# A gated recurrence with its 256 pairs of time steps written out, turned into a loop on each engine that holds two pairs, with the transfers cut to one pair each

## The reference

```python
Xz = einsum('btc,hc->tbh', X, Wxz) + bxz      # and Xr, Xh in the same way
def step(H, xs):
    Z = sigmoid(xz + H @ Whz.T + bhz)
    R = sigmoid(xr + H @ Whr.T + bhr)
    H_tilda = tanh(xh + R * H @ Whh.T + bhh)
    H_new = Z * H + (1.0 - Z) * H_tilda
    Y = H_new @ Whq.T + bhq
    return (H_new, Y)
return x + transpose(Ys)
```

## Time and profile before

| | |
|---|---|
| time, median of 3 runs | 2449.64 us (2446.89 to 2451.39) |
| profiled execution, its own time | 2457.01 us |
| its span, first to last instruction | 2455.2 us |
| TensorE matmul busy | 2351.4 us (96%) |
| TensorE weight load busy | 2230.2 us (91%) |
| VectorE busy | 1345.5 us (55%) |
| ScalarE busy | 817.1 us (33%) |
| instructions in the trace | 177755 |
| mean granted TensorE clock | 0.998 |

### The profile page before, as it was taken

The page is one execution under the profiler, slowest core; times in us unless marked ns, Lnnn a source line. Parts: engine busy times, 40 slices in busy tenths (PEclk is TensorE's granted clock), DMA queues, the critical chain, the costliest instruction groups (busy, mean ns, idle before and its releaser), DMA issues.

```text
span 2455.2 us, 177755 instructions
## 1 busy us (share of the span) xinstructions
PE 2351.4 (96%) x81984; PEld 2230.2 (91%) x81984; DVE 1345.5 (55%) x8961; ACT 817.1 (33%) x4610; POOL 0.8 (0%) x6
## 2 busy tenths in 40 slices
PE   8999999999999999999999999999999999999999
PEld 7999989999999999899999899989999898988898
DVE  3555555555555555555555555555555555555555
ACT  2333333333333333333333333333333333333333
POOL 0000000000000000000000000000000000000000
PEclk9999999999999999999999999999999999999999
DMA  4000000000000000000000100000000000000000
GB/s 165 30 22 22 22 30 30 30 13 22 30 30 30 13 30 22 30 30 13 30 22 30 30 23 21 22 30 30 30 13 22 30 30 30 13 22 30 30 13 13
DMA packets 16491, 69.53 MB, mean 28 GB/s; under 512 B 2304, under 2 KB 2432, under 8 KB 14848
## 3 DMA queue, kind: packets, MB, share of 16 engines
q1 hardware_dynamic: 15744, 58.17, 6.7%
HBM read 41.39 MB, written 16.78 MB: 24 GB/s over the span
## 4 chain that ended last, share of the span: by engine, by line
PE 95%; issue 4%; DMA 1%; SPq 0%; DVE 0%; ACT 0%
PE pre L180 57%; PE pre L147 29%; PE y_bank L159 9%; DMA wh<-in_w_hh 1%; SPq L110 0%; SPq L112 0%; DVE pre_t L269 0%; DVE fresh L305 0%; SPq L118 0%; DVE reset_state L294 0%; ACT cand L258 0%; SPq L116 0%; ACT z_not L254 0%; DVE states L309 0%; DVE kept L299 0%
## 5 line engine op out<-in xcount | busy, mean ns | idle before, releaser
L180 PE MATMUL pre<-wh,states 128*16 128x128 f32 x32768 | 1093.4, 273 | 22.7 <-issue 13.4
L147 PE MATMUL pre<-wx,xt 128*32 128x128 f32 x24576 | 1034.6, 273 | 67.9 <-issue 63.7
L269 DVE STREAM_TRANSPOSE pre_t<-pre 128x32 f32<-128x32 f32 (+2 forms) x3584 | 618.4, 216 | 801.8 <-PE pre L180 767.1
L180 PEld LDWEIGHTS pre<-wh,states 128*16 128x16 f32 x32768 | 949.9, 104 | 68.3 <-issue 60.8
L147 PEld LDWEIGHTS pre<-wx,xt 128*32 128x32 f32 x24576 | 814.3, 110 | 120.0 <-issue 117.2
L180 PE MATMUL pre<-wh,reset_state 128*16 128x128 f32 (+1 forms) x16384 | 616.8, 273 | 6.9 <-issue 5.5
L251 ACT ACTIVATE r_gate<-pre_t 128x16 f32<-128x16 f32 (+1 forms) x1536 | 234.5, 215 | 1003.1 <-DVE pre_t L269 1003.1
L180 PEld LDWEIGHTS pre<-wh,reset_state 128*16 128x16 f32 (+1 forms) x16384 | 473.0, 103 | 29.3 <-issue 27.8
L258 ACT ACTIVATE cand<-pre_t 128x16 f32<-128x16 f32 (+1 forms) x1536 | 234.8, 215 | 327.6 <-DVE pre_t L269 327.6
L159 PE MATMUL y_bank<-wq,states 128*32 128x128 f32 x8192 | 299.7, 273 | 1.5 <-DVE states L309 1.5
L159 PEld LDWEIGHTS y_bank<-wq,states 128*32 128x32 f32 x8192 | 258.0, 110 | 1.8 <-DVE states L309 1.8
(11 more groups left out here) (11 smaller groups left out, 10.5 us busy)
## 6 DMA issues: line engine op xcount, KB each, us to landing
xt<-in_x_t SPq DMA_DIRECT2D x32, 512.0 KB, 3.4
y_io<-in_x_res SPq DMA_DIRECT2D x32, 512.0 KB, 3.3
out<-y_io SPq DMA_DIRECT2D x32, 512.0 KB, 2.8
wx<-in_w_xr SPq DMA_DIRECT2D x1, 1024.0 KB, 5.8
wx<-in_w_xz SPq DMA_DIRECT2D x1, 1024.0 KB, 6.0
wx<-in_w_xh SPq DMA_DIRECT2D x1, 1024.0 KB, 8.2
wh<-in_w_hr SPq DMA_DIRECT2D x1, 1024.0 KB, 11.0
wh<-in_w_hz SPq DMA_DIRECT2D x1, 1024.0 KB, 12.9
```

The costliest lines, as they stand in the source:

```text
L147: mm = nc.tensor.matmul(pre[k % 2][Q * j:Q * (j + 1), g, 0:P], xt[:, n % 2, tp, m, :], wx[g][:, m, P * j:P * (j + 1)], start=False, stop=( ...
L180: mm = nc.tensor.matmul(pre[k % 2][Q * j:Q * j + rows, g, 0:P], of, wh[g][:, m, P * j:P * (j + 1)], start=False, stop=(m == G - 1), skip_g ...
L269: nc.vector.transpose(flat(pre_t[g][:, a:b]), pre[k % 2][:, g, Q * a:Q * b]).then_inc(done, 1)
```

## The change

Each engine's program becomes a hardware loop (`Fori`) whose body is one turn: pairs 2i and 2i+1. The first turn is written out ahead of the loop and the last one behind it, so the loop runs over i = 1 to 126. Semaphores still count up through the whole kernel, so a wait inside the loop is against a value worked out from the loop's register (`k = 2 * i + par`, `t = 2 * k + s`). Buffer halves are chosen by `par`, which is a constant in the body. The transfers of `xt`, `y_io` and `out` are now one pair each (64 KB instead of 512 KB), with their addresses in the chip's main memory worked out from the loop's register. The work on TensorE, VectorE and ScalarE and its order are the same.

```diff
+        def pair_loop(eng, pair):
+            for par in range(2):
+                pair(0, par, first=True, last=False)
+            with eng.Fori(1, turns - 1) as i:
+                for par in range(2):
+                    pair(i, par, first=False, last=False)
+            for par in range(2):
+                pair(turns - 1, par, first=False, last=True)
@@ sync @@
+            def pair(i, par, first, last):
+                k = 2 * i + par
+                if not last:
+                    sp.wait_ge(xt_used, k + 1)
+                    load_xt(k + 2, par)
+                if not (first and par == 0):
+                    sp.wait_ge(y_added, k)
+                    sp.dma_start(out[k - 1], y_io[:, 1 - par]).then_inc(stored[1 - par], 16)
+                    if not (last and par == 1):
+                        sp.wait_ge(stored[1 - par], 16 * (i + par))
+                        load_res(k + 1, 1 - par)
-            for n in range(tiles):
-                if n + 2 < tiles:
-                    sp.wait_ge(xt_used, n + 1)
-                    load_xt(n + 2)
-                sp.wait_ge(y_added, PAIRS * (n + 1))
-                sp.dma_start(out[n], y_io[:, n % 2]).then_inc(stored[n % 2], 16)
-                if n + 2 < tiles:
-                    sp.wait_ge(stored[n % 2], 16 * (n // 2 + 1))
-                    load_res(n + 2)
@@ tensor @@
-                if tp == PAIRS - 1 and g == H and end == G:
+                if g == H and end == G:
                     mm.then_inc(xt_used, 1)
+            def pair(i, par, first, last):
+                k = 2 * i + par
+                more = not (last and par == 1)
+                start = first and par == 0
+                recur(R, 2 * k, par, 0, start)
+                recur(Z, 2 * k, par, 0, start)
+                if more:
+                    pe.wait_ge(xt_loaded[1 - par], 16 * (i + 1 + par))
+                    pe.wait_ge(pre_filled, k + 2)
+                    project_x(1 - par, R, 0, 1)
+                recur(H, 2 * k, par, 0, start)
...
@@ vector @@
+            def add_y(k, par, loads):
+                dve.wait_ge(y_loaded[par], 16 * loads)
                 dve.wait_ge(y_projected, k + 1)
```

More of the change, by code:

```diff
@@ L24, in gru @@
 def gru(nc, x_t, x_res, h0, w_x, w_h, w_q, b_gate, b_out, out):
-    tiles = x_t.shape[0]
-    pairs = tiles * PAIRS
+    pairs = x_t.shape[0]
+    turns = pairs // 2
     with ExitStack() as ctx:
@@ L92, in flat, with state_of, load_xt, load_res @@
             return t.rearrange("p m b -> p (m b)")
-        def state_of(k, s):
-            return states[:, (k + 1) % 2, :, 2 * B:3 * B] if s == 0 else states[:, k % 2, :, B:2 * B]
+        def state_of(par, s):
+            return states[:, 1 - par, :, 2 * B:3 * B] if s == 0 else states[:, par, :, B:2 * B]
+        def pair_loop(eng, pair):
[6 more added lines that the diff above has]
+                pair(turns - 1, par, first=False, last=True)
         @block.sync
         def _(sp):
[L100 to L106, removed]
+            def load_xt(k, par):
+                sp.dma_start(xt[:, par], x_t[k]).then_inc(xt_loaded[par], 16)
+            def load_res(k, par):
+                sp.dma_start(y_io[:, par], x_res[k]).then_inc(y_loaded[par], 16)
+            def pair(i, par, first, last):
[9 more added lines that the diff above has]
+                        load_res(k + 1, 1 - par)
+            load_xt(0, 0)
             sp.dma_start(wx[R][:], w_x[R]).then_inc(wx_loaded[R], 16)
@@ L119, in _ @@
             sp.dma_start(wq[:], w_q).then_inc(wq_loaded, 16)
-            load_res(0)
-            load_xt(1)
-            load_res(1)
-            for n in range(tiles):
-                if n + 2 < tiles:
-                    sp.wait_ge(xt_used, n + 1)
-                    load_xt(n + 2)
-                sp.wait_ge(y_added, PAIRS * (n + 1))
-                sp.dma_start(out[n], y_io[:, n % 2]).then_inc(stored[n % 2], 16)
-                if n + 2 < tiles:
-                    sp.wait_ge(stored[n % 2], 16 * (n // 2 + 1))
-                    load_res(n + 2)
-            for n in range(2):
-                sp.wait_ge(stored[n], 16 * (tiles // 2))
+            load_xt(1, 1)
+            load_res(0, 0)
+            load_res(1, 1)
+            pair_loop(sp, pair)
+            sp.wait_ge(y_added, pairs)
+            sp.dma_start(out[pairs - 1], y_io[:, 1]).then_inc(stored[1], 16)
+            for par in range(2):
+                sp.wait_ge(stored[par], 16 * turns)
         @block.gpsimd
@@ L183, in recur @@
                 mm.then_inc(pre_done[g], 1)
+            def pair(i, par, first, last):
[9 more added lines that the diff above has]
+                recur(H, 2 * k, par, 0, start)
+                if not start:
+                    if first:
+                        pe.wait_ge(wq_loaded, 16)
+                    project_y(k - 1, 1 - par)
+                if more:
+                    project_x(1 - par, R, 1, G)
+                recur(R, 2 * k + 1, par, 1)
+                recur(Z, 2 * k + 1, par, 1)
+                if more:
+                    project_x(1 - par, Z, 0, 1)
+                recur(H, 2 * k + 1, par, 1)
+                if more:
+                    project_x(1 - par, Z, 1, G)
+                    project_x(1 - par, H, 0, G)
             pe.wait_ge(zeroed, 2)
@@ L199, in _, with fill_pre, fill_y, pair @@
                 project_x(0, g, 0, G)
[L201 to L225, removed]
+            pair_loop(pe, pair)
             for h in range(N):
                 pe.wait_ge(state_ready[h], 2 * pairs + 1)
-            project_y(pairs - 1)
+            project_y(pairs - 1, 1)
         @block.scalar
         def _(act):
[L232 to L237, removed]
+            def fill_pre(par):
+                nc.scalar.copy(pre[par][:, :, 0:P], bias_rows[:]).then_inc(pre_filled, 1)
+            def fill_y(k, par, first):
+                if not first:
                     act.wait_ge(y_added, k - 1)
[L239 to L245, removed]
+                nc.scalar.copy(y_bank[par][:, 0:P], bias_out[:]).then_inc(y_filled, 1)
+            def pair(i, par, first, last):
+                k = 2 * i + par
                 for s in range(2):
@@ L260, in _, with turn, pair @@
                     if s == 0:
-                        fill_y(k)
-                    elif k + 2 < pairs:
-                        fill_pre(k + 2)
+                        fill_y(k, par, first)
+                    elif not last:
+                        fill_pre(par)
+            act.wait_ge(bias_ready, 1)
+            act.wait_ge(banks_primed, 1)
+            fill_pre(0)
+            fill_pre(1)
+            pair_loop(act, pair)
         @block.vector
         def _(dve):
-            def turn(g, k, part, done):
+            def turn(g, par, part, done):
                 a, b = part
[L269 to L274, removed]
+                nc.vector.transpose(flat(pre_t[g][:, a:b]), pre[par][:, g, Q * a:Q * b]).then_inc(done, 1)
+            def add_y(k, par, loads):
+                dve.wait_ge(y_loaded[par], 16 * loads)
                 dve.wait_ge(y_projected, k + 1)
-                nc.vector.tensor_tensor(y_io[:, n % 2, tp, :], y_bank[k % 2][:, 0:P], y_io[:, n % 2, tp, :], ALU.add
+                nc.vector.tensor_tensor(y_io[:, par, :], y_bank[par][:, 0:P], y_io[:, par, :], ALU.add
                                         ).then_inc(y_added, 1)
[L279 to L284, removed]
+            def pair(i, par, first, last):
+                k = 2 * i + par
                 for s in range(2):
                     t = 2 * k + s
-                    old, new = state_of(k, s), state_of(k + s, 1 - s)
+                    old, new = state_of(par, s), state_of(par if s == 0 else 1 - par, 1 - s)
                     dve.wait_ge(pre_done[R], t + 1)
                     for h in range(N):
-                        turn(R, k, PARTS[h], r_turned[h])
+                        turn(R, par, PARTS[h], r_turned[h])
                     for h, (a, b) in enumerate(PARTS):
@@ L296, in _ @@
                     dve.wait_ge(pre_done[Z], t + 1)
-                    turn(Z, k, (0, G), z_turned)
+                    turn(Z, par, (0, G), z_turned)
                     dve.wait_ge(z_ready, t + 1)
@@ L310, in _ @@
                                                 ).then_inc(state_ready[h], 1)
-                    if s == 1 and k > 0:
-                        add_y(k - 1)
-            add_y(pairs - 1)
+                    if s == 1 and not (first and par == 0):
+                        add_y(k - 1, 1 - par, i + par)
+            dve.wait_ge(bias_loaded, 8 * 16)
+            nc.vector.tensor_tensor(bias_rows[:], bias_in[:, 0], bias_in[:, 1], ALU.add).then_inc(bias_ready, 1)
+            dve.wait_ge(h0_loaded, 16)
+            for h in range(N):
+                dve.sem_inc(state_ready[h], 1)
+            pair_loop(dve, pair)
+            add_y(pairs - 1, 1, turns)
 _W = "L0_cond_"
@@ L326 @@
     batch, steps, chans = x.shape
-    tiles = steps // TS
+    pairs = steps // 2
```

(4 more changed lines are left out.)

37 lines of the change are left out of this document (14 added, 23 removed).

## The result

The changed kernel takes 2266.84 us (median of 4 runs, 2266.62 to 2266.93), against 2449.99 us before (4 runs, 2446.89 to 2451.39): the ratio is 0.9254, with a 95% interval of 0.9238 to 0.9270. The forecast was 2270 us. The span of the profiled execution fell from 2455.2 to 2264.9 us, by 190.3 us.

What follows compares the result with a forecast made beforehand. TensorE was taken as the bound, with 195 us of gaps at instruction block edges. 2455.2 - 190 + 13 - 3.2 = 2275, + 1.8 - 7.4 = 2269.4, say 2270 us; likeliest case 2255 to 2300, 8 in 10 reaching up to 2590 us.

Steps and rivals of the forecast that it cites:

- What bounds the kernel: TensorE: 195 us of its span are gaps where it ran dry at edges of 256-instruction blocks.
- Instruction blocks, -190 us: TensorE's loop body stays in the core after its first time round, so edges bring no packet: -190 us.
- code that runs once: First turn, first time through the body and last turn, 3 of 128 turns, keep their gaps; the term scales by 125/128.
- The branch, +13 us: Each engine's add, compare and jump, 126 times, costs 0.1 us a turn: +13 us, bounds nothing to 55 us.
- Waits against registers, 0 with 184 us as the upper end: Register waits on VectorE, ScalarE and TensorE cost 0; 184 us if handovers tripled.
- Transfers by pair, 0: SyncE's smaller transfers cost nothing: `xt` arrives about 7 us after the pair's end, needed at 10.5 us.
- rival 3: TensorE's blocks don't stay but jumps are covered, or edges cost the same; only bursts go: 2405 to 2530 us, chance 0.10.
- Start and end, -3.2 us: Smaller first `xt` load ahead of the weights gives -2.7 us, smaller last store -0.5 us.
- The sum: Span 2455.2 - 190 + 13 - 3.2 = 2275 us; + 1.8 - 7.4 for execution time and median gives 2269.4 us.
- 1: Handovers between engines get longer, but by less than the gain: 2295 to 2410 us, chance 0.15.
- 4: Register waits cost over 0.06 us each, or VectorE's or ScalarE's body is refetched each turn: 2454 to 2640 us, chance 0.11.
- 2: TensorE's backward branch misses and waits for a packet each turn, 1.1 to 2.4 us: 2600 to 2765 us, chance 0.17.

Runs made afterwards that it cites:

- experiment 4: Changed kernel with four pairs in the loop body instead of two, 63 rounds: 2754.11 us, ratio 1.1296 to the kernel before.
- experiments 10: Changed kernel with 48 more small unneeded matmuls a pair in the loop, body about 1675 instructions: 3394.34 us.
- experiment 11: Changed kernel with 80 more small unneeded matmuls a pair in the loop, body about 1931 instructions: 4793.07 us.
- experiment 2: Changed kernel with only TensorE's program a loop, VectorE, ScalarE and SyncE written out with waits against constants: 2267.27 us.
- experiment 1: Changed kernel with the loop written out again, leaving only the transfers by pair: 2419.33 us, ratio 0.9928 to the kernel before.
- experiment 3: Changed kernel with all engines but TensorE looping: 2417.95 us, beside 2419.33 us for everything written out.
- experiment 7: Changed kernel with the 8 projection loads between the Z and H products moved behind the H product, in both steps: 2350.47 us.
- Experiment 8: Changed kernel with the second pair's input load issued ahead of the state weights: 2263.89 us, against 2267.03 us run beside it.

## Why the prediction was right, step by step

*What bounds the kernel.* Right: 195 us of gaps, from the pace of one quiet pair against the mean, and all of them at block edges. The changed kernel runs at the quiet pair's pace throughout.

*Instruction blocks, -190 us.* Right in mechanism and size. By spans the whole change is 190.3 us. The start lost 28.79 - 25.41 = 3.4 us (the second step's R product, changed kernel against the kernel before), the end gained about 1.1 us (from the last `add_y` to the end of the span 3.1 us before, 2.0 us after), so the gaps gave 190.3 + 3.4 - 1.1 = 192.6 us. The 5 us that I kept for code that runs once were mostly not needed. Whether blocks stay was the open condition, taken on an argument and not from a row; experiments 4, 10 and 11 show that it is one of size. The jump back over some 5 blocks brought no packet in its turns (15 in the whole run), nor did that over 6.5 (17); the one over 7.5 went with 9 a turn. The room for 8 blocks and the block fetched ahead behind the loop's end, with which the expectations of experiments 10 and 11 reckon, were my assumptions, and no run shows them: about 1675 instructions stayed and about 1931 did not.

*The branch, +13 us.* Too much. 18329 matmuls in every 500 us leave nothing for it, though TensorE's loop adds some 8 instructions a turn (179884 in the trace of experiment 2, 178875 in that of experiment 1). It is the term that was off by the most, all of its 13 us. The profile shows 168 edges without a gap, not what covered them; the instructions already queued were my inference.

*Waits against registers, 0 with 184 us as the upper end.* The value held; experiment 3 shows no price even where the loop's other effects are absent, and the handover took 0.04 us. Whether the engines read the registers ahead of the waits no view shows. No run made the handovers longer, so the 184 us stay an estimate. What experiment 7 shows is that the chain is as tight as the estimate supposed: without the 0.22 us of cover in each step the kernel takes 84 us more.

*Transfers by pair, 0.* Right in the loop. Each lands in 1.6 to 1.8 us (the profile page's medians), so `xt` is there about 4.5 us after the end of the pair, where I had reckoned with 7 and had 10.5. The 48 us for bursts in rival 3 were too high: smaller transfers alone gave 0.7%, 10 to 26 us.

*Start and end, -3.2 us.* Wrong, and the one step with the wrong sign: it came out at +2.3 us. I counted the bytes that no longer stand ahead of the weights, but not that one tile of `xt` used to hold 8 pairs. Now the second pair has a load of its own, behind all weights on SyncE's queue, and TensorE waits 3.33 us for it. Experiment 8 shows it by taking the wait away. The term for the smaller first load had the right sign: the first R product started at 17.57 us instead of 18.23, but that is 0.7 us and not 2.7. The 165 GB/s were the mean of a slice of 61 us, while from 10 to 25 us the kernel before moved 412 GB/s, at which 448 KB are 1.1 us:

```profile
10.00:25.00 15.00, 9.12 (x224) 6.65 (x224) 2.03 (x13) 3.27 (x12) 0.00 (x0) 0.77 1.02 412
```

Reading `load_xt(1, 1)` against the place where `xt_loaded` is first waited for would have found the wait.

*The sum.* -192.6 + 0 + 2.3 against -190 + 13 - 3.2: the forecast span was 2275 us, the measured one 2264.9. The 7.4 us between the profiled execution before and its median, which I carried over, did not return: the changed kernel's median (2266.84) is its profiled time. The two errors, +10 and -7, nearly cancel. That is luck, and it makes 2270 look closer than the working was. The 190 us hold for the profiled execution of the kernel before, which was a slow one (2457.01 us); beside the experiments its medians were 2434.32 to 2453.14 us, against which 2266.84 us are a gain of 167 to 186 us.

*The rivals.* 1 and 4 are out by experiments 2 and 3 and by VectorE's and ScalarE's 3 instruction packets, 3 by the 15 of TensorE. 2 didn't happen here but happens with a body twice as long (experiment 4), at 4.5 us and a granted clock of 0.51 over 3.2 us instead of the 1.1 to 2.4 us that I had put, and with one half as long again (experiment 11).

## What to carry to other kernels

```profile
1207.60 3.19 PEld L214 LDWEIGHTS pre<-wq 128*32 128x32 f32 x96
```

- The clock also fell where TensorE never stood still. With 48 of them a pair the weight loads are busy for all of 500 us, and the mean granted clock is 0.89, where the changed kernel without them has 1.00:

```profile
500.00:1000.00 500.00, 500.00 (x15742) 500.00 (x15735) 200.63 (x1324) 120.53 (x681) 0.00 (x0) 0.89 0.05 15
```
